# Expert blocks: the four transposes of a block's rows at the head of its own program instead of amid its predecessor's up products

## What is computed

```python
# layer 0: 8 experts, the 4 best of each row; layer 1: 8 experts, the 2 best, with biases
h = gelu(x @ up_w[e])              # 256 -> 1024
y = h @ down_w[e]                  # 1024 -> 256
out = x + tanh(g) * sum_over_chosen(weight[row, e] * y)
```

## Time and profile before

| | us |
|---|---|
| median of 3 runs (lowest, highest) | 1445.96 (1443.44, 1447.94) |
| span of the profiled execution | 1437.5 |
| TensorE busy in it | 1368.0 (95%) |
| VectorE busy | 768.2 (53%) |
| ScalarE busy | 737.5 (51%) |
| GpSimd busy | 484.3 (34%) |

### The profile page before, as it was taken

One profiled execution on the slowest core, in us unless ns is written; L12 is line 12 of the kernel. 1 busy time (PEld: TensorE's weight loads), 2 busy tenths in 40 slices (PEclk: granted clock), 3 DMA queues, 4 the chain that ended last, 5 costly groups with the idle time before them and its releaser, 6 DMA issues. The chain is left out here.

```text
span 1437.5 us, 25731 instructions
## 1 busy us (share of the span) xinstructions
PE 1368.0 (95%) x9996; PEld 1260.1 (88%) x9996; DVE 768.2 (53%) x1667; ACT 737.5 (51%) x1403; POOL 484.3 (34%) x378
## 2 busy tenths in 40 slices
PE   6999999999998999999999999899999988999997
PEld 5976966967865999999999999799999978999996
DVE  5555666666566453552553423466676774456422
ACT  4354444453444555555555545345544454666554
POOL 0100100000001664655665544202111136667553
PEclk9999999999998999999999999999999999999998
DMA  6111022031023553553553333312123155565332
GB/s 235 41 38 63 16 91 62 16 93 61 18 78 98 136 149 48 149 149 53 146 148 60 57 55 62 98 45 79 57 83 107 31 186 155 130 164 138 61 55 39
DMA packets 73680, 127.57 MB, mean 89 GB/s; under 512 B 7952, under 2 KB 53664, under 8 KB 73504
## 3 DMA queue, kind: packets, MB, share of 16 engines
q1 hardware_dynamic: 46816, 81.92, 17.3%
q0 software_dynamic: 26688, 43.34, 15.8%
HBM read 100.44 MB, written 24.79 MB: 87 GB/s over the span
## 5 line engine op out<-in xcount | busy, mean ns | idle before, releaser
L2526 DVE TENSOR_TENSOR m_hidden_lo<-m_act_out,m_hidden_hi 128x512 fp32r<-128x512 f32 x224 | 154.8, 692 | 352.1 <-ACT m_hidden_hi L2466 341.5
L428 PE MATMUL banks<-m_down_hi,m_hidden_hi 128*128 128x256 f32 x896 | 258.5, 289 | 1.2 <-DVE m_hidden_lo L2526 0.8
L428 PE MATMUL banks<-m_down_lo,m_hidden_hi 128*128 128x256 f32 x896 | 256.1, 286 | 2.2 <-issue 2.2
L428 PE MATMUL banks<-m_down_hi,m_hidden_lo 128*128 128x256 f32 x896 | 255.9, 286 | 0.0
L428 PE MATMUL banks<-m_xt_hi,m_up_hi 128*128 128x256 f32 x640 | 184.2, 288 | 1.4 <-DVE m_xt_lo L2509 1.4
L428 PE MATMUL banks<-m_xt_hi,m_up_lo 128*128 128x256 f32 x640 | 180.9, 283 | 0.0
L428 PE MATMUL banks<-m_xt_lo,m_up_hi 128*128 128x256 f32 x640 | 180.8, 282 | 0.0
L428 PEld LDWEIGHTS banks<-m_down_hi,m_hidden_hi 128*128 128x128 f32 x896 | 172.3, 192 | 4.3 <-DVE m_hidden_lo L2526 1.0
L428 PEld LDWEIGHTS banks<-m_down_lo,m_hidden_hi 128*128 128x128 f32 x896 | 172.2, 192 | 2.6 <-issue 2.6
L428 PEld LDWEIGHTS banks<-m_down_hi,m_hidden_lo 128*128 128x128 f32 x896 | 172.0, 192 | 0.0
L2466 ACT ACTIVATE m_hidden_hi<-m_act_out 128x512 fp32r<-128x512 f32 x224 | 141.6, 632 | 7.1
(11 more groups left out here) (396 smaller groups left out, 3511.0 us busy)
## 6 DMA issues: line engine op xcount, KB each, us to landing
stage<-in_up SPq DMA_DIRECT2D x22, 512.0 KB, 5.1
stage<-in_down SPq DMA_DIRECT2D x21, 512.0 KB, 4.1
stage<-in_ctx_rows SPq DMA_DIRECT2D x20, 512.0 KB, 3.8
stage<-in_ctx_cols SPq DMA_DIRECT2D x24, 402.0 KB, 3.8
m_stage<-in_down SPq DMA_DIRECT2D x10, 512.0 KB, 4.9
m_stage<-in_up SPq DMA_DIRECT2D x9, 512.0 KB, 5.2
rows<-xn SPq DMA_DIRECT2D x8, 528.0 KB, 3.5
stage<-in_ctx_picked SPq DMA_DIRECT2D x8, 512.0 KB, 4.4
```

The source lines that it names most:

```text
L428: mm = q.e.matmul(dst, a, b, start=first and n == 0, stop=last and n == 2, skip_group_check=True)
L2526: q.e.tensor_tensor(lo, m.act[(n * HP + h) % ACTS], f32(hi), ALU.subtract).then_inc(*hidden_lo.mark((layer, n, h)))
```

## The change

In every block (e, j) with j of 1 or more, other than (0, 1), the transposes of its rows, their high part on ScalarE and the weight copy and low part on VectorE move from the predecessor's program to the head of the block's own, behind the branch that decides whether the block exists. On TensorE they stand ahead of the 48 down products, on ScalarE ahead of the scaling of y, on VectorE ahead of the first low part. Those of (e + 1, 0) and of (0, 1) stay where they are. GpSimd's program has the same text. No wait is added or removed; waits move with what they guard.

```diff
@@ tensor_ups
                 if n == 0:
                     continue
-                if h == (1 if j else 0) and j + 1 < NB:
-                    tensor_turn_block(q, layer, e, j + 1)
                 if h == 2 and j == always(e) and e + 1 < E:
                     tensor_turn_block(q, layer, e + 1, 0)
@@ tensor_block
             n = numbered(e, j)
             if j and n > 1:
+                tensor_turn_block(q, layer, e, j)
                 for f in range(HT):
                     tensor_down(q, layer, n - 1, e, f)
@@ scalar_block
+            if j and n > 1:
+                scalar_turn_block(q, layer, e, j)
             scalar_y(q, layer, n - 1, weights_of_before(m, e, j))
             for h in range(HP):
                 scalar_pair(q, layer, e, j, h)
-                if h == (1 if j else 0) and j + 1 < NB:
-                    scalar_turn_block(q, layer, e, j + 1)
@@ vector_block
             if j == 0:
                 convert(q, "d", ahead(layer, e - 1))
+            elif n > 1:
+                vector_turn_block(q, layer, e, j)
             for h in range(HP):
                 vector_low(q, layer, e, j, h)
-                if h == (1 if j else 0) and j + 1 < NB:
-                    vector_turn_block(q, layer, e, j + 1)
```

## The result

The kernel after takes 1458.57 us (median of 6 runs, 1455.24 to 1466.58), the kernel before 1446.95 us (6 runs, 1443.44 to 1452.65). The ratio is 1.0069, 95% interval 1.0038 to 1.0099: about 10 us slower by the ratio (5 to 14), 11.6 by the medians, where 1.2 us faster was forecast and 1451.5 was the upper end of the range. The profiled execution of the kernel after has a span of 1453.4 us, against 1437.5; the runs list 2 us more than the span of the same execution.

What follows compares the result with a forecast made beforehand. TensorE was taken as the bound, busy 426.24 of 430 us in layer 0's experts. Terms -6.9 + 2.8 + 2.0 + 0.9 = -1.2 us took 1445.96 to about 1444.8 us, range 1439.5 to 1451.5.

Steps and rivals of the forecast that it cites:

- Removed sets: TensorE at expert ends: 16 unused sets of four transposes go, 0.43 us each, 6.9 us off.
- The new place at nothing: TensorE at block heads: the 38 moved and kept sets cost 0 in their new place.
- VectorE's cover in (2, 1): VectorE in block (e, 1): the rows' low part is ready 0.5 to 1.1 us before the ups; cost 0.
- that rival (0.04): VectorE late in (e, 1): low part misses the ups, +7 us for half a us beyond the cover, 1452; chance 0.04.
- GpSimd 3.5 us later: GpSimd at expert ends: the unwanted last gather starts 3.5 us later, and the queue behind it moves along.
- Step (a): y of (e, 0) at openings: ScalarE held 2.8 us, within 4.49 us of idle time; cost to TensorE taken as 0.
- The rival: GpSimd becomes the bound at each opening: TensorE stands at the next downs, +8 us, 1453; chance 0.12.
- Step (b): Rows of (7, 0) in layer 1: their gather comes late and TensorE waits 2.8 us, bounds 0 and 4.5.
- Step (c): End of layer 0: late gather holds the normalisation and TensorE at attention 1 by 2.0 us, bounds 0.5 and 3.3.
- (d): End of the kernel: the late gather delays the last add by 0.9 us, bounds 0 and 2.
- Code loading: Rival: the instruction stall at an end branch goes or one arises, -4 or +4 us, 1441 or 1449; chance 0.10.
- The base: Starting point: profiled span 1437.5 us, with the 8.5 us by which the runs' median lay above it carried over.

Runs made afterwards that it cites:

- sets_amid: Kernel before with one more set of four identity transposes amid the ups in each of 38 blocks, no wait added; 1462.91 us, ratio 1.0091.
- after_own: Kernel after with the gather of (e, j + 3) moved to the head of GpSimd's next block, behind the branch; 1445.64 us, ratio 0.9973 to the kernel before.
- before_own: Kernel before, transposes unmoved, with the gather of (e, j + 3) moved to the head of GpSimd's next block; 1445.53 us, ratio 0.9976.
- sets_head: Kernel before with one more set of four transposes at the head of 38 blocks, behind an added wait for the rows' low part; 1473.14 us, ratio 1.0175.
- gate_last: Kernel before, GpSimd made to wait for the block's last low part of hidden values ahead of the gather of (e, j + 3); 1457.1 us, ratio 1.0058.
- the second execution: Kernel before, unchanged, profiled once more (before_again); 1446.84 us over 8 runs, profiled span 1442.9 us.
- before_small: Kernel before with the weight loads of experts 3 to 7 cut to an eighth of their bytes, only layer 0 comparable; 1487.67 us.
- after_small: Kernel after with the weight loads of experts 3 to 7 cut to an eighth of their bytes, only layer 0 comparable; 1493.75 us.

## Why the prediction was wrong

- **Removed sets: right.** Block ends of layer 0 show -0.36 us and -0.08 behind it, 0.44 a set for the 0.43 forecast; sets_amid gives the same price from the other side. In layer 1 most of them went inside distances that grew; they show alone at experts 6 and 7 (-0.5 and -0.4).
- **The new place at nothing: right for TensorE.** In layer 0 the distances inside an expert are unchanged to 0.03 us with a set moved in each. VectorE's cover in (2, 1) was forecast at 0.5 to 1.1 us; its low part ended 0.7 us ahead of the ups (592.31, 592.97). In after_own the cover was gone in three blocks (e, 1), so that rival (0.04) was not far off.
- **GpSimd 3.5 us later: right** where it starts (3.4 at the end of layer 0). **Step (a) failed.** Its mis-sized term is the wait for the landing, "4.9 us; it moves along": moved by 3.5 us the gather came among the weight loads and took 8.1 to 9.8 us at five of layer 0's ends. The slip was 2.8 to 6.8 us in nine openings where 2.8 was forecast for all, the room of 3.1 us (3.5 estimated) was passed in eight of the 13 that have a block (e, 1), and 0 us became 9 in layer 0 and 8 in layer 1, falls of the clock among them. The rival named the mechanism and nearly the threshold; its chance of 0.12 and its 8 us were too low, since I gave 0.7 us of slower landings no cause, and the loads were one.
- **Step (b): right in mechanism for this kernel, too small.** One new wait, at the place named, 3.5 us for 2.8 forecast; with the clock 5.2. (The other of the two above, 2.3 us at layer 1's start, reads 1.7 before.) It missed that the moved copy alone holds the same rows as long (after_own). "The wait of (b) is one gap like that of 924, so I add nothing" failed: behind 3.5 us of idle time the clock stood at 0.50 for 3 us.
- **Step (c)** gave 0.9 us for 2.0 in the distance across attention 1, and **(d)** 1.8 for 0.9, both inside their bounds. In after_own and before_own the last add is back at 7.0 us behind the product, and yet the end is as late as in the kernel after (+1.9 and +2.0); why is open.
- **Code loading.** The end of expert 6 and the opening of 7 in layer 0 became 4.0 us shorter, and it did so in every kernel with the change (4.0 to 4.9), but also by 4.0 in sets_amid and sets_head and by 2.1 in gate_last. What the stall hangs on is open; its going hides as much of the loss. (The chances take 0.03 of this rival beyond each bound, where a third of 0.05 is 0.02.) That of the earlier trace rows stayed, as a wait of 3.1 us.
- **The base.** The profiled execution before ran 1437.5 us, and 2 us are added to a span. I carried 8.5 us over and took it for overhead; 6.5 of it said that this was an unusually good execution. All margins of step (a) were read from it. Its one opening in the earlier trace rows had 4.49 us of idle time and no slip; others in it had slips of 0.8 to 1.1 us in layer 1, and in the second execution up to 3.9.

Not shown by experiment: that the loads do in layer 1 what they do in layer 0, since before_small and after_small can't be compared there. The kernel after's trace fits it: the same distance is 8.1, 8.1, 8.3 and 8.6 us at the ends of experts 0 to 3, where loads start some 1 us behind the gather, and 5.6 at that of expert 4, where they start 3.4 us behind it, and 6.0 at that of expert 6, which has none. Not tried: how the openings go with both the gather order and an earlier release of y.

## What to carry to other kernels

When a wait moves later on a queue, look up what else will be under way at the new time: a transfer's duration belongs to its moment, and the one read from a quiet moment was the least that it could take here. An operation for work that is not wanted must be taken out of every queue at once; taking the transposes out and leaving the gather in GpSimd's queue made the gather later. And compare the span of a profiled execution with the runs before its margins are trusted: if it is faster than they are, its room is too.

## What the runs showed of the hardware

- A gather of two halves of 128 rows took 9.8 us from its first issue to the release of its buffer with the DMA engines at 0.94 to 1.04, 6.8 us in the same place with the loads cut, 5.2 us ahead of them. At the two ends without loads (share 0.24) it took 5.7 and 5.0.
- TensorE's clock fell behind single gaps of 2.0, 3.45, 3.5 and 3.8 us (behind the last, which ended at 1315.80, it was 0.72 in 1316 to 1322) and not behind one of 1.4. The kernel after, TensorE's gaps and windows behind them:

```profile
762.78 0.39 PE L428 MATMUL banks<-m_down_hi,m_hidden_hi 128*128 128x256 f32 x1 [1.36 <-DVE m_hidden_lo L2525]
...
1247.44 0.50 PE L2324 MATMUL banks<-b,m_own 16*128 16x256 f32 x2 [2.04 <-DVE m_hidden_lo L2525]
```

```profile
762.00:768.00 6.00, 5.22 (x43) 5.22 (x44) 3.59 (x8) 3.84 (x8) 4.81 (x4) 1.00 0.54 86
1248.00:1250.00 2.00, 2.00 (x14) 2.00 (x15) 1.37 (x4) 1.97 (x6) 1.70 (x2) 0.75 0.45 69
1250.00:1254.00 4.00, 4.00 (x26) 4.00 (x26) 1.60 (x4) 1.28 (x3) 2.35 (x3) 0.70 0.51 60
```

Each fall cost 1.4 to 1.7 us beside its gap, with the unused sets reckoned in. In the kernel before, the pauses of 924 to 926 left the clock at 1.00, which I had taken for the rule.
